# SiLU stays in its PSUM bank, and GpSimd takes some of the subtractions that split activations and w2

## The reference, cut to what matters

```python
x = x + xattn(layernorm(x), ctx, Wq, Wk, Wv, Wo)      # scores normalised by mean and variance over a batch, softmax
x = x + ffn(layernorm(x), ...)
# ffn, for each token:
cw   = top-2 of softmax(x @ gate_w + gate_b), zero for the other experts      # 8 routed experts
a, b = split(x @ w1[e] + b1[e])                       # 128 features to 2 x 128
out  = sum over e of cw[e] * ((silu(a) * b) @ w2[e] + b2[e]) + shared expert (weight 1)
```

## Time and profile before

| what | value |
|---|---|
| time, median of 3 runs | 135.35 us (135.25 to 135.39) |
| the profiled execution: time, span | 135.15 us, 133.4 us |
| PE busy (share of the span) | 127.5 us (96%) |
| DVE busy | 107.6 us (81%) |
| ACT busy | 84.8 us (64%) |
| POOL busy | 23.9 us (18%) |
| granted TensorE clock | 1.00 throughout |

### The profile page before, as it was taken

How to read it: one execution, slowest core, us unless ns; L and a number is a source line. 1 busy time by engine, 2 the same in 40 slices (tenths; PEclk the granted TensorE clock), 3 DMA queues, 4 the chain that set the end, 5 groups by cost and what they waited for, 6 DMA issues and landing times.

```text
span 133.4 us, 2135 instructions
## 1 busy us (share of the span) xinstructions
PE 127.5 (96%) x632; PEld 96.7 (72%) x632; DVE 107.6 (81%) x313; ACT 84.8 (64%) x165; POOL 23.9 (18%) x41
## 2 busy tenths in 40 slices
PE   7899999889999999999999999999999999999992
PEld 7677796858577776686788676598677667788871
DVE  1497788696997989999759997699697879989872
ACT  1557978996265389947653299956633987647250
POOL 7184154057700020602100020001200000000000
PEclk9999999999999999999999999999999999999999
DMA  3999400002910000098000002087000207910022
GB/s 107 304 331 269 149 7 0 0 2 86 337 59 0 0 0 2 10 296 328 0 5 0 0 0 79 18 292 332 2 0 0 79 5 182 403 44 5 0 79 79
DMA packets 8828, 12.97 MB, mean 97 GB/s; under 512 B 1321, under 2 KB 6994, under 8 KB 8306
## 3 DMA queue, kind: packets, MB, share of 16 engines
q1 hardware_dynamic: 8242, 12.62, 28.1%
q10 hardware_dynamic: 576, 0.23, 0.6%
HBM read 11.73 MB, written 1.11 MB: 96 GB/s over the span
## 4 chain that ended last, share of the span: by engine, by line
PE 61%; issue 15%; DVE 9%; ACT 7%; POOL 6%; DVEq 0%; POOLq 0%; ACTq 0%
PE bank L998 55%; ACT prob L508 3%; POOL w_rest L434 3%; POOL ln_rstd L419 2%; PE bank L1062 1%; PE bank L1014 1%; ACT L553 1%; PE bank L1113 1%; PE bank L1090 1%; DVE x L902 1%; ACT act_head L580 1%; PE bank L1181 1%; DVE g_beats L824 1%; DVE g_rank L827 1%; ACT silu L588 1%
## 5 line engine op out<-in xcount | busy, mean ns | idle before, releaser
L588 ACT ACTIVATE silu<-bank,b_cols 128x512 f32<-128x512 f32 (+1 forms) x37 | 24.8, 676 | 23.7 <-PE bank L998 23.2
L998 PE MATMUL bank<-x_head,w_head 128*128 128x512 f32 x72 | 33.7, 468 | 0.3 <-issue 0.3
L998 PE MATMUL bank<-x_head,w_rest 128*128 128x512 f32 x72 | 28.5, 395 | 0.0
L998 PE MATMUL bank<-x_rest,w_head 128*128 128x512 f32 x72 | 28.5, 395 | 0.0
L881 DVE SCALAR_TENSOR_TENSOR act<-bank,b_cols,silu 128x512 f32<-128x512 f32 (+1 forms) x34 | 24.9, 734 | 1.3 <-DVE silu L873 0.3
L873 DVE TENSOR_TENSOR silu<-silu,cw_all 128x512 f32<-128x512 f32 (+1 forms) x28 | 18.6, 668 | 3.3 <-ACT silu L588 2.6
L998 PE MATMUL bank<-act,w_sb 128*128 128x512 f32 x38 | 19.4, 592 | 0.0
L998 PEld LDWEIGHTS bank<-x_head,w_head 128*128 128x128 f32 x72 | 13.6, 189 | 5.3 <-issue 2.7
L998 PEld LDWEIGHTS bank<-x_rest,w_head 128*128 128x128 f32 x72 | 13.6, 189 | 3.9 <-issue 1.9
L998 PEld LDWEIGHTS bank<-x_head,w_rest 128*128 128x128 f32 x72 | 13.5, 188 | 3.3
L890 DVE TENSOR_TENSOR act_rest<-act,act_head 128x512 fp32r<-128x512 f32 x15 | 10.0, 685 | 4.1 <-ACT silu L588 2.0
(11 more groups left out here) (130 smaller groups left out, 219.4 us busy)
## 6 DMA issues: line engine op xcount, KB each, us to landing
cw_all<-cw_dram SPq DMA_DIRECT2D x4, 1024.0 KB, 7.0
cw_all<-cw_dram SPq DMA_DIRECT2D x4, 512.0 KB, 5.0
cw_all<-cw_dram SPq DMA_DIRECT2D x6, 256.0 KB, 3.7
x_sb<-in_x_dram SPq DMA_DIRECT2D x4, 256.0 KB, 4.2
w_sb<-in_L_ffn_rw_dram SPq DMA_DIRECT2D x1, 1024.0 KB, 7.4
ctx_sb<-in_ctx_dram SPq DMA_DIRECT2D x4, 192.0 KB, 4.2
out_dram<-x SPq DMA_DIRECT2D x3, 256.0 KB, 2.1
w_sb<-in_L_ffn_rw_dram SPq DMA_DIRECT2D x1, 512.0 KB, 7.1
```

Source lines behind the costliest of these rows:

```text
L588: scalar.activation(silu[:, k, cols], hid(n, 0)[:, cols], ACT.Silu, bias=b1_cols[:, 0, e:e + 1]).then_inc(silu_sb, 1)
L998: return pe.matmul(dst, lhs, rhs, start=start, stop=stop, skip_group_check=True)
```

## The change

SiLU: where `in_bank(n)` holds (slots 4 to 8, 11 to 17, 20 to 26 and 29 to 34) ACT writes SiLU back into the PSUM bank of a, and DVE's product reads it there and writes to SBUF. TensorE may then reuse a's bank only when the product is done, not when SiLU is done. The first routed expert of chunks 1 to 3 keeps its unweighted result in b's bank.

Down: six more slots are divided: 4, 12, 13, 21, 22 and 33. The rests of 4, 12, 13, 21 and 22 (`BY_POOL`) are subtracted by GpSimd, in two halves of 256 columns each, behind heads that ACT makes ahead of its SiLU two slots later. DVE does the rest of slot 33 on top of the 15 that it had.

w2: ACT makes the heads in slot 2, and GpSimd makes the rests (640 and 512 columns) in slot 3; DVE's 1152-column subtraction is gone. The second of GpSimd's power steps for the scores moves behind the rests (`scores_rstd`).

```diff
-        POOL_AT = {'first_rstd': [-9, 1], 'scores_rstd': [-2, 0], 'second_rstd': [4, 0]}
+        POOL_AT = {'first_rstd': [-9, 1], 'scores_rstd': [-1, 1], 'second_rstd': [4, 0]}
...
-        DIVIDED = [n for n in range(NX - 1, LAST - STRAIGHT)
-                   if n >= NX * (C - 1) or n % NX in ((0, 1, 2, 7, 8) if n < NX * 2 else (0, 7, 8))]
+        DIVIDED_OF = [(4, 8), (0, 1, 2, 3, 4, 7, 8), (0, 3, 4, 7, 8), range(NX - STRAIGHT)]
+        DIVIDED = [n for n in range(NX * C) if n % NX in DIVIDED_OF[n // NX]]
+        BY_POOL = [n for n in DIVIDED if n < NX * (C - 1) and n % NX in (3, 4)]
+        BY_DVE = [n for n in DIVIDED if n not in BY_POOL]
...
-            return {7: "first", 2: "last"}.get(m % NX, "between")
+            return {3: "first", 4: "first", 7: "first", 2: "last"}.get(m % NX, "between")
...
+        def in_bank(n):
+
+            return FOUR_BANKS_FROM <= n < LAST and n % NX >= (1 if n < NX else 2)
...
+            def w2_rests():
+                for g, (lo, hi) in enumerate(W2_GROUPS):
+                    pool.wait_ge(w2_head_sb, g + 1)
+                    pool.tensor_tensor(w2_rest[:, lo:hi, :], w2_sb[:, lo:hi, :], w2_head[:, lo:hi, :].bitcast(F32), ALU.subtract).then_inc(w2_rest_sb, 1)
+
+            def act_rests(m):
+                pool.wait_ge(act_head_sb, divided(m))
+                for cols in (slice(0, N // 2), slice(N // 2, N)):
+                    pool.tensor_tensor(act_rest[:, m % 3, cols], act[:, m % 4, cols], act_head[:, m % 3, cols].bitcast(F32), ALU.subtract).then_inc(pool_rest_sb, 1)
...
+                if n == 3:
+                    w2_rests()
+                for m in pool_rests_in(n):
+                    act_rests(m)
...
-                    scalar.activation(silu[:, k, cols], hid(n, 0)[:, cols], ACT.Silu, bias=b1_cols[:, 0, e:e + 1]).then_inc(silu_sb, 1)
+                    silu_out = hid(n, 0)[:, cols] if in_bank(n) else silu[:, k, cols]
+                    scalar.activation(silu_out, hid(n, 0)[:, cols], ACT.Silu, bias=b1_cols[:, 0, e:e + 1]).then_inc(silu_sb, 1)
...
-                if n in (5, 6):
-                    w2_heads(n - 5)
+                if n == 2:
+                    w2_heads(0)
+                    w2_heads(1)
...
-                        dve.tensor_tensor(silu[:, k, cols], silu[:, k, cols], cw_all[:, e - 1, cols], ALU.mult).then_inc(scaled_sb, 1)
+                        dve.tensor_tensor(silu[:, k, cols], hid(n, 0)[:, cols] if in_bank(n) else silu[:, k, cols], cw_all[:, e - 1, cols], ALU.mult).then_inc(scaled_sb, 1)
...
-                if n == NX:
-                    w2_rests()
...
-                    pe.wait_ge(silu_sb, n - 1)
+                    if in_bank(n - 2):
+                        pe.wait_ge(scaled_sb, weighted(n - 2))
+                    else:
+                        pe.wait_ge(silu_sb, n - 1)
...
-                    pe.wait_ge(w2_rest_sb, 1)
-                    pe.wait_ge(act_rest_sb, divided(n))
+                    pe.wait_ge(w2_rest_sb, len(W2_GROUPS))
+                    if n in BY_POOL:
+                        pe.wait_ge(pool_rest_sb, 2 * (BY_POOL.index(n) + 1))
+                    else:
+                        pe.wait_ge(act_rest_sb, BY_DVE.index(n) + 1)
```

More of the change, by code:

```diff
@@ L171, in xattn_moe_kernel @@
         act_sb, raw_act_sb, y_ps = sem("act_sb"), sem("raw_act_sb"), sem("y_ps")
-        act_head_sb, act_rest_sb = sem("act_head_sb"), sem("act_rest_sb")
+        act_head_sb, act_rest_sb, pool_rest_sb = sem("act_head_sb"), sem("act_rest_sb"), sem("pool_rest_sb")
         out_ps, outt_sb, tok_ps, final_sb = sem("out_ps"), sem("outt_sb"), sem("tok_ps"), sem("final_sb")
@@ L318, in parts_place, with heads_in, pool_rests_in, dve_rests_in @@
                 return "between"
-            return {7: "first", 2: "last"}.get(m % NX, "between")
-        def divided_in(n, places):
-            return [m for m in range(n - 2, n) if m in DIVIDED and parts_slot(m) == n and parts_place(m) in places]
+            return {3: "first", 4: "first", 7: "first", 2: "last"}.get(m % NX, "between")
+        def heads_in(n, places):
+            return [m for m in DIVIDED if parts_slot(m) == n and parts_place(m) in places]
+        def pool_rests_in(n):
+            return [m for m in BY_POOL if parts_slot(m) == n]
+        def dve_rests_in(n, places):
+            return [m for m in BY_DVE if parts_slot(m) == n and parts_place(m) in places]
+        def weighted(n):
+            c, e = n // NX, n % NX
+            return E * c + e - c
+        def in_bank(n):
+            return FOUR_BANKS_FROM <= n < LAST and n % NX >= (1 if n < NX else 2)
         def downs_in(n):
@@ L662, in _ @@
                     pieces[piece](k)
-                for m in divided_in(n, ("first",)):
+                for m in heads_in(n, ("first",)):
                     act_heads(m)
@@ L666, in _ @@
                     expert_silu(c, e)
-                for m in divided_in(n, ("between",)):
+                for m in heads_in(n, ("between",)):
                     act_heads(m)
@@ L674, in _ @@
                     pieces[piece](k)
-                for m in divided_in(n, ("last",)):
+                for m in heads_in(n, ("last",)):
                     act_heads(m)
-                if n in (5, 6):
-                    w2_heads(n - 5)
+                if n == 2:
+                    w2_heads(0)
+                    w2_heads(1)
             out_bias(C - 1)
@@ L856, in first_expert_gate @@
                 dve.wait_ge(b_ps, n + 1)
+                dve.scalar_tensor_tensor(hid(n, 1)[:, :], hid(n, 1)[:, :], b1_cols[:, 1, 1:2], silu[:, k, :], ALU.add, ALU.mult).then_inc(raw_act_sb, 1)
+                between()
                 dve.wait_ge(y_ps, n - 3)
-                dve.scalar_tensor_tensor(act[:, n % 4, :], hid(n, 1)[:, :], b1_cols[:, 1, 1:2], silu[:, k, :], ALU.add, ALU.mult).then_inc(raw_act_sb, 1)
-                between()
                 dve.wait_ge(cw_in[cw_group(1)], 16 * arrivals(c, cw_group(1)))
                 dve.wait_ge(raw_act_sb, c)
-                dve.tensor_tensor(act[:, n % 4, :], act[:, n % 4, :], cw_all[:, 0, :], ALU.mult).then_inc(act_sb, 1)
+                dve.tensor_tensor(act[:, n % 4, :], hid(n, 1)[:, :], cw_all[:, 0, :], ALU.mult).then_inc(act_sb, 1)
             def expert_gate(c, e, between):
@@ L876, in expert_gate @@
                     if e >= 1:
-                        dve.wait_ge(scaled_sb, E * c + e + h - c)
+                        dve.wait_ge(scaled_sb, weighted(n) + h)
                     dve.wait_ge(b_ps, n + 1)
@@ L882, in expert_gate @@
                                              ALU.add, ALU.mult).then_inc(act_sb, 1)
-            def w2_rests():
-                dve.wait_ge(w2_head_sb, len(W2_GROUPS))
-                dve.tensor_tensor(w2_rest[:, :, :], w2_sb[:, :, :], w2_head[:, :, :].bitcast(F32), ALU.subtract).then_inc(w2_rest_sb, 1)
             def act_rests(n):
@@ L977, in between @@
                 def between():
-                    for m in divided_in(n, ("first", "between")):
+                    for m in dve_rests_in(n, ("first", "between")):
                         act_rests(m)
@@ L985, in _ @@
                     expert_gate(c, e, between)
-                for m in divided_in(n, ("last",)):
+                for m in dve_rests_in(n, ("last",)):
                     act_rests(m)
```

## The result

The changed kernel takes 137.74 us (median of 4 runs, 137.55 to 138.12), beside 135.37 us for the kernel before (135.25 to 135.43). The ratio is 1.018 [1.016, 1.020]: 2.4 us slower, inside the range of 135.3 to 139.7 and 0.9 us under the forecast of 138.6. The profiled span grew from 133.4 to 135.7 us, at a granted TensorE clock of 1.0 in both.

A forecast was written before the change was run, and what follows sets the result against it. TensorE's work was taken to set the time, except at 50.9 and 81.3, where VectorE does. Terms -0.31 + 0.83 + 1.3 + 1.5 = +3.3 us gave 138.6 us, range 135.3 to 139.7.

The forecast's parts named there:

- GpSimd beside VectorE: GpSimd subtractions hold VectorE instructions with two SBUF inputs, up to a whole half (0.73 us) per meeting; full holds 40%.
- First stretch: VectorE work from 41.34 to the wait at 50.9: w2 rests leave 0.5 us, slot 4's halves add 0.8; +1.3 us.
- Second stretch: Rests of slots 12 and 13 meet the tiny statistics two or three times before the wait at 81.3; +1.5 us.
- Savings of 4, 12 and 13 lost: These divided downs save 0.16 us each, but TensorE waits that much longer for the `cw_cols` transposes at 50.9 and 81.3.
- Where TensorE pays: TensorE waits for VectorE at the router's transposes of `cw_cols`, at 50.9 and 81.3.
- Third chunk: Only divided downs 21 and 22 keep their saving, as the wait at 107.08 has 0.67 us to spare; -0.31 us.
- The end: Down 33 must wait for its rest behind VectorE's product of slot 34, delaying slot 35 and the last downs; +0.83 us.
- No hold: Rival: GpSimd doesn't hold VectorE, leaving +0.5 us, 135.4 to 136.1; 20%.
- Partial holds: Rival: one meeting per stretch, or reads over well before the instruction ends; +1.2 to +2, 136.5 to 137.3; 15%.
- Worse order: Rival: second w2 piece gets ahead of slot 3's product, and TensorE waits for router inputs in slot 5; 140 or more; 10%.
- Faster: Rival: VectorE's stretches ahead of two transposes shorten through earlier SiLU or quicker bank products; -0.4 us, 134.9; 13%.
- The signs: Profile after: float32 downs 38 to 26, `ln_shift` 1.3 us late, statistics spread, transposes 1.3 and 2.8 later, down 33 over 0.8 behind.

The follow-up runs named there:

- e2: The changed kernel with every GpSimd subtraction replaced by two memsets of the same size, so GpSimd writes but doesn't read: 135.53 us, ratio 1.0006.
- e3: The changed kernel with downs 4, 12 and 13 whole and w2 subtracted by VectorE in slot 9: 135.83 us, ratio 1.0027.
- e9: The changed kernel with downs 4, 12, 13 and 33 whole, w2 on VectorE in slot 9 and SiLU in SBUF: 135.30 us, ratio 0.9985.
- e4: The changed kernel with SiLU written to SBUF as before the change: 137.92 us, ratio 1.0207 to the kernel before.
- e8: The changed kernel with downs 4, 12, 13 and 33 whole, w2 on VectorE in slot 9, SiLU in its bank: 135.06 us, ratio 0.9982.
- e1: The changed kernel with the down of slot 33 as one float32 matmul again: 137.20 us, ratio 1.0139.

## Why the prediction was right, and where its sizes were off

- **GpSimd beside VectorE** was the term that decided, and the mechanism was as predicted: `ln_shift` started on time but lasted 1.33 us instead of 0.15, until the first w2 piece ended, and the tiny statistics lasted until the halves ended. Rows before had shown GpSimd held by VectorE only; that VectorE is held too was an inference, and it held. The Trainium skill ("SBUF — State Buffer", section "Who interferes with whom") also says that GpSimd's writes don't take part; e2 agrees, with `sim_sq` at 0.17 us inside a memset.
- **First stretch, predicted +1.3, measured +1.01.** `x_rest` starts 17.20 us behind slot 0 before and 17.51 after, so 0.31 us of `ln_shift`'s hold is left, not 0.5. The tiny ones lose 0.72, not 0.8. Most of the miss lies in the length of the hold on `ln_shift`: 1.33 us was predicted and 1.18 measured (1.33 less its own 0.15), for it ends with the GpSimd piece and doesn't begin then. What was absorbed ahead of `x_rest` was nearly as predicted, 0.87 us against 0.83.
- **Second stretch, predicted +1.5, measured +1.25.** There were three meetings, the upper number: `sim_sq`, `sim_ex` and the last `sim_mom` are longer by 0.34, 0.49 and 0.42. They sum to 1.25. The halves started at 72.64, which is the predicted 71.7 and the first stretch's lateness to 0.1 us. Three meetings were priced at 1.8 and two at 1.2; no meeting cost a whole half of 0.73, because a tiny instruction's own 0.17 us and the gap ahead of it lie inside the half too.
- **Savings of 4, 12 and 13 lost:** shown. e2 (divided) and e3 (whole) have the same two stretches within 0.01 us.
- **Where TensorE pays** was incomplete. The prediction named the transposes of `cw_cols` alone. The profile has most of the wait at the score averages, two slots earlier, which the trace puts down to the router's logits. The sum holds all the same: with the holds gone (e2) the first average follows its down without a wait, and the stretches as a whole have the length of before.
- **Third chunk, predicted -0.31, measured -0.50.** Divided downs 21 and 22 give 0.26 (before 25.81, e9 25.55). The other 0.24 is the bank (e4 and e9 25.55, after and e8 25.31), which the prediction had at nothing. It weighed the bank by the lengths of the products alone, and left out its own row of a power held for 0.38 us by a product with two SBUF inputs. With SiLU in the bank that hold is gone, and by the lines of e8 and e9 the whole 0.25 us at `x_rest` follows from there, but for a few hundredths by which ACT's SiLU is shorter. This is the one term that the prediction left out.
- **The end, predicted +0.83, measured +0.75:** shown by e1, the rest of slot 33.
- **The rivals.** "No hold" falls with the lengths above. "Partial holds" came nearer to the time than to the cause: there were six holds on the way to the two waits, the five on the statistics and the one on `ln_shift`, and all lasted to the end of the GpSimd instruction. A seventh, on `g_z` beside the rests of 21 and 22 (0.25 us instead of 0.19), cost nothing, as predicted. "Worse order" needed the second w2 piece ahead of the product of slot 3; the product got in first. "Faster" wanted shorter VectorE stretches; with holds taken out (e2) they have the length of before, to 0.03 us. Products from a bank take 686 ns, those of before 688, so the 0.3 us for dearer PSUM sources were rightly left out.
- **The signs.** The float32 downs fell from 38 to 26 instructions, and down 33 starts about 0.8 us behind the end of the a tile of slot 35 (127.61 and three passes of 0.23 us, then 129.13). `sim_sq` to the last `sim_mom` spread over 1.37 and 1.90 us. The transposes are 1.0 and 2.3 us later, counted from slot 0, where 1.3 and 2.8 were named, and `ln_shift` isn't late in starting but long.
- **Sum.** The predicted +3.3 us stands against +2.51 by the four columns; 0.29 of the miss is the first stretch, 0.25 the second, 0.19 the third chunk, 0.08 the end. The stretches come out too long because the prediction charged the GpSimd time in full and didn't take off the VectorE instruction's own time inside it; the errors all point one way, and none cancelled another.

## What to carry to other kernels

A subtraction that is "free" on GpSimd has to be put where VectorE isn't about to run instructions with two SBUF inputs; six halves cost 2.0 us here at one moment, and nothing once four of them stood just behind those instructions and two ahead of them. Before an engine is given less work in some slots, look whether it waits behind those slots: three of six divided downs here saved nothing, and a fourth, at the end, cost 0.75 us. When instruction counts stay and busy time grows, compare the lengths of the smallest instructions first.

## What the runs showed of the hardware that was not expected

- ACT's SiLU from one bank into the same bank is 28 ns shorter than into SBUF, as the groups by form show, after and then before:

```profile
L620 ACT ACTIVATE bank<-bank,b_cols 128x512 f32<-128x512 f32 x25 | 16.5, 659 | 20.3 <-PE bank L1025 20.1
```

```profile
L588 ACT ACTIVATE silu<-bank,b_cols 128x512 f32<-128x512 f32 x35 | 24.0, 687 | 21.8 <-PE bank L998 21.4
```

- The tiny power on GpSimd (128x8) doesn't hold VectorE as a subtraction of 256 columns does: `sim_sq` took 0.17 us inside the one and 0.40 and 0.51 beside the other. Yet a power is held by VectorE's product with two SBUF inputs (the 128x4 one took 1.39 against 1.01 us).
- In this kernel lateness doesn't carry from one chunk to the next: over eleven profiles the stretch from the first to the second cw transposes was 30.3 or 31.6 us, whatever the one ahead of it had done.
